# A mixture-of-experts layer: bfloat16 rank counts, padding rows ahead of a wait, epsilon inside the root

## What is computed

```python
def _moe(x, wg, w1, b1, w2, b2):                      # 8 experts, cap = 1024 rows each
    gates = softmax(xf @ wg)
    idx = argmax(gates)
    mask1 = one_hot(idx, E)
    loc = sum((cumsum(mask1, 0) - 1.0) * mask1, -1)   # the row's rank in its expert
    keep = loc < cap
    disp[idx * cap + loc] = xf                         # rows sorted by expert
    h = disp @ w1[e] + b1[e]
    y = h @ w2[e] + b2[e]
    out = where(keep, gate_val * y[slot], 0.0)
y1 = _ln(x + _mha(x, ...))                             # attention within 16 rows, 4 heads
y2 = _ln(y1 + _moe(y1, ...))                           # _ln divides by sqrt(var + eps)
x = x + 0.5 * y2
```

## Time and profile before

| | us |
|---|---|
| median of three runs | 2509.3 |
| the profiled execution's own time | 2509.4 |
| its span, first to last instruction | 2507.7 |
| TensorE busy | 2231.7 (89%) |
| VectorE busy | 1929.4 (77%) |
| ScalarE busy | 1569.3 (63%) |
| GpSimd busy | 919.2 (37%) |
| mean granted TensorE clock | 0.95 |

### The profile page before, as it was taken

How to read it: one execution, slowest core, us unless ns; L and a number is a source line. 1 busy time by engine, 2 the same in 40 slices (tenths; PEclk the granted TensorE clock), 3 DMA queues, 4 the chain that set the end, 5 groups by cost and what they waited for, 6 DMA issues and landing times. The chain is left out here.

```text
span 2507.7 us, 47389 instructions
## 1 busy us (share of the span) xinstructions
PE 2231.7 (89%) x15250; PEld 1330.2 (53%) x15252; DVE 1929.4 (77%) x5490; ACT 1569.3 (63%) x3207; POOL 919.2 (37%) x1158
## 2 busy tenths in 40 slices
PE   6999997977389889999999999999987999998474
PEld 4666666866155534444444444444465666666363
DVE  4677776589598788889888898998845677776496
ACT  2555554256144459999999999999941455554263
POOL 1577787036354400000000000000011387777166
PEclk7999998998699979999999999999998999999796
DMA  4233252856268424454444444444245122322673
GB/s 119 77 122 114 86 200 95 282 190 194 84 203 208 143 56 95 94 96 93 93 89 89 96 93 95 96 93 88 46 134 177 34 85 85 102 104 71 217 225 101
DMA packets 233752, 298.79 MB, mean 119 GB/s; under 512 B 43150, under 2 KB 181457, under 8 KB 232867
## 3 DMA queue, kind: packets, MB, share of 16 engines
q1 hardware_dynamic: 206483, 235.82, 36.8%
q0 software_dynamic: 17152, 50.49, 5.3%
q10 hardware_dynamic: 9872, 9.45, 1.2%
HBM read 203.36 MB, written 100.60 MB: 121 GB/s over the span
## 5 line engine op out<-in xcount | busy, mean ns | idle before, releaser
L2288 DVE CUSTOM_DVE_ANT_0 banks<-banks,ahead_bias 128x128 f32<-128x128 f32 (+7 forms) x1024 | 760.4, 776 | 94.1 <-PE banks L1997 80.5
L2203 ACT ACTIVATE attn_probT<-banks 128x512 f32<-128x512 f32 x1152 | 623.0, 608 | 72.3 <-PE banks L2014 61.8
L1997 PE MATMUL banks<-ahead_kst,ahead_qst 96*128 96x512 bf16 (+3 forms) x1536 | 425.9, 337 | 12.1 <-DVE attn_low L2288 7.4
L2014 PE MATMUL banks<-ahead_qst,ahead_kst 99*128 99x256 bf16 (+3 forms) x2176 | 394.9, 280 | 6.7 <-ACT banks L2194 1.3
L2345 POOL CAST attn_lowp<-attn_lowT 128x32 bf16<-128x32 f32 x64 | 13.4, 209 | 848.1 <-DVE attn_lowT L2296 848.1
L2036 PE MATMUL banks<-attn_probT,ahead_vb 128*32 128x256 f32 (+3 forms) x4352 | 315.6, 400 | 8.8 <-ACT attn_probT L2203 8.3
L2194 ACT COPY banks<-ahead_biasT 128x512 f32<-128x512 f32 x480 | 281.2, 611 | 16.3 <-PE banks L2052 6.6
L1997 PEld LDWEIGHTS banks<-ahead_kst,ahead_qst 96*128 96x128 bf16 x1536 | 118.9, 97 | 264.5 <-DVE attn_low L2288 174.3
L2014 PEld LDWEIGHTS banks<-ahead_qst,ahead_kst 99*128 99x128 bf16 x2176 | 180.8, 98 | 140.4 <-ACT attn_probT L2203 43.5
L438 PE MATMUL banks<-ffn_xT,winT 128*128 128x512 f32 x512 | 250.6, 613 | 4.6 <-DVE ffn_w L756 1.7
L977 POOL TENSOR_TENSOR ffn_w1T<-ffn_ring,own 128x512 f32<-128x512 f32 x128 | 134.4, 1062 | 176.5 <-PE banks L475 102.6
(11 more groups left out here) (259 smaller groups left out, 3955.3 us busy)
## 6 DMA issues: line engine op xcount, KB each, us to landing
ffn_ring<-disp SPq DMA_DIRECT2D x144, 257.0 KB, 3.2
ahead_qst<-qparts SPq DMA_DIRECT2D x384, 64.0 KB, 2.8
ahead_kst<-kparts SPq DMA_DIRECT2D x192, 128.0 KB, 5.0
ffn_ring<-in_L_attn_x_dram SPq DMA_DIRECT2D x32, 512.0 KB, 5.1
ffn_w<-in_L_ffn_w_dram SPq DMA_DIRECT2D x16, 1024.0 KB, 9.3
ahead_bias<-neard SPq DMA_DIRECT2D x128, 128.0 KB, 2.2
ahead_biasT<-neardT SPq DMA_DIRECT2D x128, 128.0 KB, 5.7
ffn_ring<-x SPq DMA_DIRECT2D x32, 512.0 KB, 4.9
```

What stands on the lines that cost most here:

```text
L1997: mm = nc.tensor.matmul(score[k % 2][:, a:e], qst[0:K6, u, half, hh, ii * P:(ii + 1) * P], kst[0:K6, u, hh, a:e], start=True, stop=True)
L2014: mm = nc.tensor.matmul(tbank[t % 3][:, at:at + nb * P], kst[:, u, hh, j * P:(j + 1) * P], qst[:, u, half, hh, x:x + nb * P], start=(k == ...
L2203: nc.scalar.activation(probT[:, g % 2, i, 0:w], tbank[t % 3][:, 0:w], ACT.Exp, scale=-1.0).then_inc(s_exp, 1)
L2288: nc.vector.tensor_tensor_reduce(out=part, in0=part, in1=bias[:, hh, T - w:T], scale=1.0, scalar=BIG, op0=ALU.add, op1=ALU.min, accum_out= ...
```

## The change

Three edits, all in the feed-forward layer.

First, the counting products of `ranks` take bfloat16 operands. VectorE copies the group's counts, `tally[:, n]` (128x64), to a bfloat16 tile of two buffers, `wholeb`, at the end of `counted`, behind a wait for its own sums and, from the third group on, for the ranks of two groups before; TensorE waits for that copy instead of the sums. The triangle and the ones are copied to bfloat16 once a layer, at its start. Counts up to 256 are exact in bfloat16.

Second, SyncE writes the padding rows before it waits for the scattered rows (`sent`), which it now does behind them and, in turn 0, behind the loads of the last experts' weights.

Third, ScalarE's root takes the variance and adds epsilon itself, through a bias tile; VectorE's addition and its wait go.

```diff
@@ ffn_attention
+    def whole(n, lo, hi):
+        return wholeb[:, n % 2, lo:hi, :].rearrange("p t e -> p (t e)")
@@ tensor: ranks
             pe.wait_ge(s_rseed, n + 1)
-            pe.wait_ge(s_hot, n + 1)
-            pe.wait_ge(s_tally, 4 * n + 5)
+            pe.wait_ge(s_whole, n + 1)
             to = rank.rearrange("p t e -> p (t e)")
-            nc.tensor.matmul(to, core.before[:, :], hot(n).rearrange("p t e -> p (t e)"), start=False, stop=False,
+            nc.tensor.matmul(to, beforeb[:, :], whole(n, 4, 8), start=False, stop=False,
                              skip_group_check=True)
-            nc.tensor.matmul(to[:, 0:NE], core.ones[:, :], tally[:, n, 3, :], start=False, stop=True, skip_group_check=True)
-            nc.tensor.matmul(to[:, NE:GT * NE], core.ones[:, :], tally[:, n, 0:3, :].rearrange("p t e -> p (t e)"),
+            nc.tensor.matmul(to[:, 0:NE], onesb[:, :], whole(n, 3, 4), start=False, stop=True, skip_group_check=True)
+            nc.tensor.matmul(to[:, NE:GT * NE], onesb[:, :], whole(n, 0, 3),
                              start=False, stop=True, skip_group_check=True).then_inc(s_rank, 1)
@@ vector: counted
+            dve.wait_ge(s_tally, 4 * n + 5)
+            if n >= 2:
+                dve.wait_ge(s_rank, n - 1)
+            nc.vector.tensor_copy(wholeb[:, n % 2, :, :], tally[:, n, :, :]).then_inc(s_whole, 1)
@@ ffn
-        zero = tile("zero", 1)
+        wholeb = tile("wholeb", 2, 8, NE, dt=BF16)
+        beforeb, onesb = tile("beforeb", P, dt=BF16), tile("onesb", P, dt=BF16)
+        zero, epsc = tile("zero", 1), tile("epsc", 1)
@@ sync
             sp.wait_ge(s_tot, 1)
-            sent(sp)
             for e in range(NE):
                 full = sp.value_load(toti[0:1, e:e + 1], min_val=0, max_val=S)
                 sp.dma_start(disp[bass.ds(full + e * REGION, P), :], pad[:, :]).then_inc(s_kept, 16)
@@
                     load_w2(sp, e)
+            sent(sp)
             sp.wait_ge(s_kept, 16 * NE)
             sp.wait_ge(s_addr, 1)
@@ scalar: root
-                act.wait_ge(s_ve, n + 1)
-                nc.scalar.activation(ve[:, u, :], ve[:, u, :], ACT.Sqrt).then_inc(s_sd, 1)
+                act.wait_ge(s_mv, n + 1)
+                nc.scalar.activation(ve[:, u, :], mv[:, u, :, 1], ACT.Sqrt, bias=epsc[:, :], scale=1.0).then_inc(s_sd, 1)
@@ vector: start of the layer
             V.memset(zero[:, :], 0.0)
+            V.memset(epsc[:, :], EPS)
+            link(V.tensor_copy(beforeb[:, :], core.before[:, :]))
+            link(V.tensor_copy(onesb[:, :], core.ones[:, :]))
@@ vector: sums
                 ins.then_inc(s_mv, 1)
-                dve.wait_ge(s_mv, n + 1)
-                nc.vector.tensor_scalar(ve[:, u, :], mv[:, u, :, 1], EPS, None, ALU.add).then_inc(s_ve, 1)
```

More of the change, by code:

```diff
@@ L320, in ffn_attention @@
     xT = xs.take(2, KB, GW)
-    tally, slot, number, eidx, ebase, zero = route
+    tally, wholeb, beforeb, onesb, slot, number, eidx, ebase, zero = route
     away, esum = wide.take(GT, NE), wide.take(GT)
@@ L332, in ffn_attention @@
         ph.sem(x) for x in ("yseed", "yps", "res", "yst", "ymv", "yrs", "ynb", "yn", "ymul", "y1", "rgate"))
-    (s_logit, s_glog, s_away, s_rex, s_cand, s_hot, s_tally, s_rank, s_part, s_slot, s_gsum, s_id, s_rseed) = (
+    (s_logit, s_glog, s_away, s_rex, s_cand, s_hot, s_tally, s_rank, s_part, s_slot, s_gsum, s_id, s_rseed, s_whole) = (
         ph.sem(x) for x in ("logit", "glog", "away", "rex", "cand", "hot", "tally", "rank", "part", "slot",
-                            "gsum", "id", "rseed"))
+                            "gsum", "id", "rseed", "whole"))
     s_prep, s_xve, s_yve = (ph.sem(x) for x in ("prep", "xve", "yve"))
@@ L1087, in ffn @@
         s_got = [ph.sem("got0"), ph.sem("got1")]
-        s_tps, s_tsb, s_zps, s_sum, s_st, s_mv, s_ve, s_sd, s_inv2, s_rs, s_norm, s_scaled, s_fin, s_marked, s_seed, s_inv, s_fac = (
-            ph.sem(x) for x in ("tps", "tsb", "zps", "sum", "st", "mv", "ve", "sd", "inv2", "rs", "norm", "scaled", "fin",
+        s_tps, s_tsb, s_zps, s_sum, s_st, s_mv, s_sd, s_inv2, s_rs, s_norm, s_scaled, s_fin, s_marked, s_seed, s_inv, s_fac = (
+            ph.sem(x) for x in ("tps", "tsb", "zps", "sum", "st", "mv", "sd", "inv2", "rs", "norm", "scaled", "fin",
                                 "marked", "seed", "inv", "fac"))
@@ L1133, in ffn @@
         attend_sync, attend_tensor, attend_scalar, attend_vector, attend_gpsimd, over_yet, sent, counted_all = ffn_attention(
-            core, Phase(core, name + "_a", ph), lend, x, disp, s_disp, turn, (tally, slot, number, eidx, ebase, zero),
+            core, Phase(core, name + "_a", ph), lend, x, disp, s_disp, turn, (tally, wholeb, beforeb, onesb, slot, number, eidx, ebase, zero),
             tables, early_loads)
```

## The result

After the change four runs took a median of 2480.6 us (2479.4 to 2481.5); the kernel before, measured beside them, 2509.6. The ratio is 0.9883, with a 95% interval of 0.9867 to 0.9898: 29.0 us faster, where 22.35 were forecast. The profiled execution took 2480.0 us, its span is 2478.3.

What follows compares the result with a forecast made beforehand. TensorE was taken to bound the routing loop, VectorE the expert loop. Ranks 9.4, loop ends 0.6 less 0.25, pads 7.2 and epsilon 5.4 sum to 22.35 us, from 2509.3 to 2487 us; range 2481 to 2498.

Steps and rivals of the forecast that it cites:

- the step that priced each layer's start at nothing: Layer starts: the constant copies and the memset lie beside VectorE's wait for the first rows and cost nothing.
- The count of 13 rounds a layer: Routing loop: of 14 rank calls inside the loop, 13 count in each of two layers, 26 x 0.36 = 9.4 us.
- The term of 0.36 us: Rank products on TensorE: bfloat16 saves 0.36 us a round (0.25 to 0.45), taking 0.056 us as load pace.
- I took 0.25: VectorE's bfloat16 copy in the routing loop: takes 0.25 us (0.1 to 0.5), hidden in 0.69 us of slack.
- Rival (d): Routing loop: GpSimd's scatters hold up the copy, making the kernel slower, 2514 or 2580 us; chance 0.05.
- 0.35 in the sum: Ends of the routing loops: net 0.6 us won in the first layer, 0.25 us lost in the second.
- 7.19 forecast: Second layer, between the loops: SyncE reads the first total 7.19 us earlier, and the whole 7.2 us reach the fetch.
- The eight pads still take 1.1 us each: Second layer's padding rows: issue and 2.65 us landing stay as before, so the last lands at 2343.4 instead of 2350.6.
- rival (b): Second layer: pads, scatters and w12's load get in each other's way, pads give 2.2 us, total 2492; chance 0.10.
- the count of 30 rounds: Expert loops: 15 groups in each layer are bound by VectorE, 30 x 0.18 = 5.4 us.
- The term of 0.18 us: Expert loop: without the epsilon addition and its wait, VectorE's next operation starts 0.18 us earlier a round (at least 0.08).
- Rival (c): Second layer, first fetch: TensorE's clock stays up across the shorter idling, saving some 2.3 us, total 2485; chance 0.05.

Runs made afterwards that it cites:

- e3_eps: The kernel before with only the epsilon moved into ScalarE's square root; ratio 0.9964, 9 us faster.
- e6_copy_only: The kernel before with the bfloat16 copy and its waits, the three rank products still reading float32; 2506.0 us, ratio 0.9991.
- e10_split_pads: The kernel after, with ScalarE issuing four of the second layer's eight padding rows and SyncE the other four; 2481.6 us, ratio 0.9890.
- e11_one_fp32: The kernel after with the eight-column product of the ranks back in float32; 2488.0 us, ratio 0.9917.
- e5_small_w12: The kernel after, loading only an eighth of the saved products ahead of the second layer's experts; 2482.4 us, ratio 0.9890.
- e12_after: The kernel after, unchanged, measured again; 2483.3 us, ratio 0.9896.
- e7_warm_before: The kernel before with unread TensorE products filling two gaps of the second layer, ahead of its first transposes and the experts' transposes; ratio 1.0003.

## Why the prediction was right or wrong

**The sum.** By the parts as the runs show them: ranks 13.2, ends 0.5, pads 3.85, epsilon 7.0, together 24.6 us, where 22.35 were forecast. The forecast of the sum was near by luck, with errors in its terms that cancel: +3.8 on the ranks, -3.35 on the pads, +1.6 on epsilon, +0.2 on the ends. By these parts alone the time would be 2485, inside the range.

What put it below is the step that priced each layer's start at nothing, so that neither the sum nor the range had a term for it. The profiles of before and after differ by 29.4 us. The other 4.8 are 3.6 (start2), 2.3 (start1), 0.8 (mid, beyond the last ranks) and 1.5 (attention, first and rest) less, against 1.4 more at the ends of the loops, beyond copy and wait, and 1.9 that the expert loops gained less than in e3_eps (all but 0.2 of it in exp2). Of start2, 3.1 us are TensorE's clock behind the first transposes, and 0.5 that these came earlier; of start1, 1.2 and 1.1. The step of start2 repeated in both profiles of either kernel, and so did some 1.1 us of the attention layer; start1 did not. No run takes any of it away by itself, so the 4.8 us are located and not explained. The second measurement of after, 2483.3, lies inside the range. The first misses it by 0.4 us, less than either the start's 3.6 us or the 3.8 by which the ranks' term was too small.

**Ranks.** The count of 13 rounds a layer and the bound by TensorE were right. The term of 0.36 us was mis-sized: 0.505, above my upper bound of 0.45. Two steps failed. The pace of bfloat16 loads is 0.03 us (194.65, 194.68, 194.71), where I took 0.056 in proportion to the durations of the loads. And I left 0.11 us for the float32 load of the following L438: it begins at 194.71 and L441's first matmul follows at 194.73, so this load no longer shows. Together 0.08 us are left where I had 0.22. By the Trainium skill (TensorE: Matmul & The Clock Gate, Weight-path perf modes) I had an estimate of 0.4 us and more; the trace gives 0.505, so it erred the same way, less.

**Copy.** Right: 0.20 us (I took 0.25), hidden. Rival (d) did not come. In after 30 of the 32 copies overlap a scatter and none took over 0.27 us; most begin 0.04 us ahead of the scatter. That the rule of the Trainium skill (SBUF — State Buffer, Who interferes with whom) can bite is seen in the one copy of 0.48 us in e6_copy_only, which ended with its scatter, and in one of 0.46 us in e10_split_pads; the copy at 408.95 us in after, and most of those in e6_copy_only, began inside a scatter and took 0.20. What separates the two is open. The held copy of e6_copy_only ended 6.9 us ahead of the ranks that read it.

**Ends of the loops.** Right in sum. The last ranks themselves take 0.11 us instead of 1.30 in the first layer (I had 0.43), 1.19 won; the time shows in "mid", which is 91.2 to 92.1 us in the seven profiles with the float32 ranks and 89.7 to 90.7 in the seven with the bfloat16 ones. From the 15th to the 16th ranks 5.12 us became 5.56 in the first layer and 5.12 became 5.35 in the second, 0.66 lost. Copy and wait alone, in e6_copy_only, make that 5.38 and 5.36; what adds the last 0.18 in the first layer wasn't traced. Together 0.5 us, for 0.35 in the sum. The rounds before it hold a stretch at half clock of their own, which goes with no part: end1 is 25.1 in both profiles of after, 23.3 in both of before and 26.4 in e3_eps, whose ranks are those of before, but 23.9 in e10_split_pads and e11_one_fp32, whose ranks are bfloat16 too.

**Pads.** The mechanism was right up to the first pad: 8.62 us behind the totals before, 1.69 after, 6.93 won (7.19 forecast). The step that failed is "The eight pads still take 1.1 us each, the last issued at 2340.8 and landed 2.65 us later". From first to last issue 7.76 us became 8.79, for the reads of the totals took up to 0.81 us instead of 0.27, and the last landed 4.48 us later: 2.86 us given back. With 0.22 more from that landing to TensorE's first transposes that leaves 3.85 us. The two profiles of before and the two of after give 2.2 to 5.3, so the 3.85 is a middle value of a piece that varies. It is rival (b), whose 2.2 us were too low. The hole that I had seen in the earlier trace rows opened when the scatters were done; pads issued 7 us earlier meet those scatters. Of the 2.9 us the load of the saved products takes at least some 1 (e5_small_w12). TensorE's wait for the first fetch was 8.93 us and not 5.4: 12.62 less the 3.85, and 0.17 more since its marks came that much earlier behind the totals.

**Epsilon.** Right in kind, and right in the count of 30 rounds. The term of 0.18 us was mis-sized: a round went from 6.66 to 6.43 us, 0.23. The reciprocal starts 0.20 us earlier, where I had 0.18, and lasts 0.15 us instead of 0.18, which the operation behind it gains as well. With the little that the second intervals gave, e3_eps makes it 7.05 us in both layers, 1.6 over the forecast. In after the second loop gained 1.7 us less, in e12_after (104.83) all of it. The trace shows where: the third interval of after took 8.17 us instead of 6.46, and TensorE's granted clock was 0.57 in it, where the same stretch of e12_after has 1.00.

```profile
2353.00:2357.00 4.00, 3.90 (x10) 3.17 (x11) 3.31 (x10) 4.00 (x11) 0.43 (x1) 0.57 0.85 234
```

**Clock.** Rival (c) asked whether TensorE's clock stays up across the shorter gap. It doesn't: the transposes take 1.97 us before and after. The clock did play a part at other places: in the starts, where I had priced the edits at nothing and never asked how many microseconds at half clock the stretch held, at the end of the first loop, and in one round of the experts.

## What to carry to other kernels

A small matmul in float32 beside large ones cost 0.20 to 0.23 us here with 8 columns as with 24; exact small integers in bfloat16 cost 0.03, and the copy that makes them is free where its engine isn't the bound. A wait that is taken out from in front of DMAs is worth what the queues can take at that moment: ask what filled them during the wait, and don't price the moved transfers by their latency in the empty queue. And where TensorE starts from idle several times, put a few microseconds of range aside for its clock, in both directions, for any edit that moves the moment of the start.

## What the runs showed of the hardware

The same 70 us of a start took 70.24 to 73.60 us, with no edit in it, and the moment at which the granted clock first rose sorts them: 6.5 to 7.2 us behind the first transposes and no second fall in 11 starts, 7.3 to 9.9 us and a second fall in 17. That the two go together is seen, which brings about which is not. In the second layer a kernel repeats its own pattern (84.03 and 83.97; 80.44 and 80.37), so that comparing a kernel with itself doesn't show this spread; comparing it with kernels edited elsewhere does. In the first layer even the same instructions differ: 73.60 and 72.86 us in the two profiles of the kernel before, and 70.34 in e7_warm_before, which is edited in the second layer alone. What sets the moment of the rise stayed open: it did not follow the transposes when they came 1.1 us later.

Twenty-four bfloat16 products of 128x512 ahead of a start raised the clock to full; after 2.80 us of idling and short transposes behind them it was at 0.50 from 1923 us on.

Padding rows of 257 KB landed 2.1 to 3.2 us after their issue in the kernel before, when the scatters had landed. Issued beside scatters and a load of 2 MB they took 4.4 to 6.2 us in after and 6.0 to 7.5 in its second profile, without most of that load 3.1 to 4.5, and 6.3 to 8.9 us when two engines issued them at twice the pace.
